# Table loads in two pieces that are split over the first tile, and each tile's sums folded on VectorE before one product of TensorE

## What is computed

```python
emb = embed_table[f_ix, x_idx]                       # n x 26 x 16
lin1 = w1_table[f_ix, x_idx].sum(axis=1, keepdims=True) + w1_bias
s = emb.sum(axis=1)
fm = 0.5 * ((s * s).sum(-1) - (emb * emb).sum(axis=(1, 2)))[:, None]
h = emb.reshape(n, F * D)
h = relu(h @ mlp_w1 + mlp_b1)
h = relu(h @ mlp_w2 + mlp_b2)
mlp_out = h @ mlp_w3 + mlp_b3
last = x0 = emb.transpose(0, 2, 1)
for W in (cin_w0, cin_w1, cin_w2):                   # three layers, K = 128
    last = einsum('ndl,ndf,klf->ndk', last, x0, W)
    feats.append(last)
cin_out = concatenate(feats, axis=-1).sum(axis=1)
return lin1 + fm + mlp_out + cin_out @ lin_w + lin_b
```

## Time and profile before

| | us |
|---|---|
| median of three runs | 621.58 (621.44 to 621.97) |
| the profiled execution's own time | 620.47 |
| its span, first to last instruction | 618.7 |
| TensorE busy | 495.0 (80%) |
| VectorE busy | 360.2 (58%) |
| ScalarE busy | 361.8 (58%) |
| GpSimd busy | 358.9 (58%) |

### The profile page before, as it was taken

One profiled execution on the slowest core, in us unless ns is written; L12 is line 12 of the kernel. 1 busy time (PEld: TensorE's weight loads), 2 busy tenths in 40 slices (PEclk: granted clock), 3 DMA queues, 4 the chain that ended last, 5 costly groups with the idle time before them and its releaser, 6 DMA issues. The chain is left out here.

```text
span 618.7 us, 7077 instructions
## 1 busy us (share of the span) xinstructions
PE 495.0 (80%) x2484; PEld 414.2 (67%) x2484; DVE 360.2 (58%) x587; ACT 361.8 (58%) x707; POOL 358.9 (58%) x379
## 2 busy tenths in 40 slices
PE   0986860000299999999999999999999999999998
PEld 0983550000188887878787878888888878787776
DVE  6710701010385858686867677685868686867556
ACT  0011701010476868686867778676868686867875
POOL 6777877730037777777777777777777777000000
PEclk9997575555599999999999999999999999999999
DMA  8944122210002222222222222222222222000000
GB/s 188 217 75 22 30 34 32 32 30 27 12 3 8 8 8 8 9 7 8 8 7 8 7 8 8 8 8 9 7 8 7 8 8 7 3 1 1 1 0 2
DMA packets 21365, 13.63 MB, mean 22 GB/s; under 512 B 12654, under 2 KB 20307, under 8 KB 21075
## 3 DMA queue, kind: packets, MB, share of 16 engines
q0 software_dynamic: 11968, 3.28, 15.4%
q1 hardware_dynamic: 5773, 7.92, 5.0%
q10 hardware_dynamic: 3590, 1.99, 1.7%
HBM read 12.97 MB, written 0.19 MB: 21 GB/s over the span
## 5 line engine op out<-in xcount | busy, mean ns | idle before, releaser
L412 POOL DMA_INDIRECT emb<-rows,idx_raw x374 | 358.5, 959 | 167.1 <-issue 117.2
L653 DVE TENSOR_TENSOR z_lo<-ps_s,z_hi 128x512 fp32r<-128x512 f32 (+1 forms) x192 | 132.0, 687 | 78.2 <-ACT ps_s L478 76.9
L471 ACT ACTIVATE z_hi<-ps_s 128x512 fp32r<-128x512 f32 (+1 forms) x192 | 114.2, 595 | 89.2 <-PE ps_s L888 88.3
L902 PE MATMUL ps_q<-z_lo,zw_hi 128*127 128x512 f32 (+1 forms) x192 | 85.9, 447 | 93.0 <-DVE z_lo L653 90.1
L478 ACT ACTIVATE ps_s<-ps_s 128x512 f32<-128x512 f32 (+1 forms) x192 | 114.0, 594 | 0.7
L902 PEld LDWEIGHTS ps_q<-z_lo,zw_hi 128*127 128x127 f32 (+1 forms) x192 | 36.6, 191 | 107.0 <-DVE z_lo L653 97.6
L903 PE MATMUL ps_q<-z_hi,zw_lo 128*127 128x512 f32 (+1 forms) x192 | 76.5, 398 | 0.0
L904 PE MATMUL ps_q<-z_hi,zw_hi 128*127 128x512 f32 (+1 forms) x192 | 76.2, 397 | 0.0
L888 PE MATMUL ps_s<-xt,pick 128*128 128x512 f32 (+1 forms) x192 | 74.7, 404 | 0.4 <-DVE xt L645 0.4
L980 PE MATMUL ps_y<-look_hi,one_hot 128*128 128x442 f32 (+1 forms) x168 | 61.1, 364 | 2.6 <-DVE one_hot L733 2.5
L981 PE MATMUL ps_y<-look_lo,one_hot 128*128 128x442 f32 (+1 forms) x168 | 59.3, 354 | 0.0
(11 more groups left out here) (165 smaller groups left out, 836.2 us busy)
## 6 DMA issues: line engine op xcount, KB each, us to landing
emb<-rows,idx_raw POOLq DMA_INDIRECT x374, 3.0
w_space<-rows SPq DMA_DIRECT2D x2, 826.5 KB
m_raw<-mlp_w SPq DMA_DIRECT2D x2, 650.0 KB
w<-cin_w SPq DMA_DIRECT2D x1, 832.0 KB, 6.8
w<-cin_w ACTq DMA_DIRECT2D x1, 832.0 KB, 13.4
w_space<-cin_w SPq DMA_DIRECT2D x1, 832.0 KB, 14.8
w_space<-cin_w ACTq DMA_DIRECT2D x1, 832.0 KB, 18.7
m_raw<-rows SPq DMA_DIRECT2D x1, 826.5 KB
```

Of the source, the lines that this page charges most:

```text
L412: pool.indirect_dma_start(emb[t % EMB][:, f, :], None, rows, bass.IndirectOffsetOnAxis(row_ix[:, t, f:f + 1], 0)).then_inc(gathered[t], 16)
L471: act.activation(z_hi[0:k, c, :], ps[0:k, :], ACT.Square)
L653: dve.tensor_tensor(z_lo[0:k, u % NC, :], ps_s[s_no(t, u) % RING][0:k, :], z_hi[0:k, u % NC, :].bitcast(F32), ALU.subtract).then_inc(lo_re ...
L902: pe.matmul(ps, hi_w, lo_x, start=(c == 0), stop=False)
```

## The change

- Each table's load goes in a DMA of 112 partitions and one of 15, in place of one of 127; the last partition stays by itself.
- The look-up by tables begins with tile 3 in place of 2 (FIRST_LOOK), so that tile 0 has no look work on TensorE and tile 2's three fields are gathered by GpSimd.
- ScalarE's table copies (`look_high`) stand behind chunks 4, 6 and 8 of tile 0, VectorE's (`look_low`) behind chunks 6, 8 and 10, no longer ahead of the tile. The copy `zw_hi` and its `zw_lo` stand ahead of tile 0's third square and `z_low`.
- `times_third` writes back into `ps_t`; a new `add_third` adds that to the sum of three quarters, ahead of the last `add_product`; a new `fold` sums the four blocks of 128 columns of `prod_sum` into `folded`. `sum_products` is one product of one column, which waits for `folds` and `looked`. TensorE's first use of `ps_t` in a tile waits for `tri_added` in place of `tri_prod`.
- The branches for a tile that isn't `joined` go; none of them ran but `copy_by_position(0)`'s and the last tile's, whose orders are kept.

```diff
+FIRST_LOOK = 3
...
-                sp.dma_start(look_raw[i][0:P - 1, :], rows[at:at + (P - 1) * COLS, :].rearrange(
-                    "(p c) r -> p (c r)", c=COLS)).then_inc(look_in[i], 16)
+                for r, r_end in ((0, 112), (112, P - 1)):
+                    sp.dma_start(look_raw[i][r:r_end, :], rows[at + r * COLS:at + r_end * COLS, :].rearrange(
+                        "(p c) r -> p (c r)", c=COLS)).then_inc(look_in[i], 16)
...
+            def look_high(i):
+                act.wait_ge(look_in[i], 48)
+                act.activation(look_hi[i][:], look_raw[i][:], ACT.Copy).then_inc(look_hi_ready, 1)
...
                     square(t, u)
+                    if t == 0 and u in LOOK_SPLIT:
+                        look_high(LOOK_SPLIT[u])
...
-            for u in range(NC):
-                square(0, u)
+            square(0, 0)
+            square(0, 1)
             act.wait_ge(za_done, 1)
             act.activation(zw_hi[:, 0, 0:NROW], ps_t[:, 0:NROW], ACT.Copy).then_inc(zw_hi_ready, 1)
-            for i in range(LOOKS):
-                act.wait_ge(look_in[i], 32)
-                act.activation(look_hi[i][:], look_raw[i][:], ACT.Copy).then_inc(look_hi_ready, 1)
+            square(0, 2)
...
-                dve.tensor_tensor(tri[:], ps_t[0:XK, :], x32[t % 2][:].rearrange("p c n -> p (c n)"),
-                                  ALU.mult).then_inc(tri_prod, 1)
+                dve.tensor_tensor(ps_t[0:XK, :], ps_t[0:XK, :], x32[t % 2][:].rearrange("p c n -> p (c n)"),
+                                  ALU.mult).then_inc(tri_prod, 1)
+
+            def add_third(t):
+                s = acc[(NQ - 2) % 2][0:XK, :]
+                dve.wait_ge(tri_prod, t + 1)
+                dve.wait_ge(q_bank_free, NQ * t + NQ - 1)
+                dve.tensor_tensor(s, ps_t[0:XK, :], s, ALU.add).then_inc(tri_added, 1)
+
+            def fold(t):
+
+                dve.wait_ge(q_bank_free, NQ * t + NQ)
                 if t:
                     dve.wait_ge(y_done, t)
+                dve.tensor_reduce(folded[0:NROW, :], prod_sum[0:NROW, :].rearrange("p (j n) -> p n j", j=QUAD), AX.X,
+                                  ALU.add).then_inc(folds, 1)
...
+                times_left(t - 1, NQ - 1)
+                times_third(t - 1)
+                add_third(t - 1)
                 z_low(t, 0)
+                add_product(t - 1, NQ - 1)
                 z_low(t, 1)
+                fold(t - 1)
+                hidden2(t - 1)
...
+            def look_low(i):
+                dve.wait_ge(look_hi_ready, i + 1)
+                dve.tensor_tensor(look_lo[i][:], look_raw[i][:], look_hi[i][:].bitcast(F32),
+                                  ALU.subtract).then_inc(look_lo_ready, 1)
...
             times_third(T - 1)
+            add_third(T - 1)
             times_left(T - 1, NQ - 1)
             add_product(T - 1, NQ - 1)
+            fold(T - 1)
...
-                for j in range(QUAD):
-                    pe.matmul(ps_y[:, YCOL + t:YCOL + t + 1], tri[:, j * P:(j + 1) * P], ones[0:XK, :],
-                              start=(j == 0), stop=False)
-                pe.wait_ge(q_bank_free, NQ * (t + 1))
-                for j in range(QUAD):
-                    mm = pe.matmul(ps_y[:, YCOL + t:YCOL + t + 1], prod_sum[0:NROW, j * P:(j + 1) * P], ones[0:NROW, :],
-                                   start=False, stop=(j == QUAD - 1))
-                mm.then_inc(y_done, 1)
+                if looked_during(t):
+                    pe.wait_ge(looked, looked_during(t))
+                pe.wait_ge(folds, t + 1)
+                pe.matmul(ps_y[:, YCOL + t:YCOL + t + 1], folded[0:NROW, :], ones[0:NROW, :],
+                          start=True, stop=True).then_inc(y_done, 1)
```

More of the change, by code:

```diff
@@ L168, in deepfm_cin_kernel @@
         prod_sum = sums[:, 2 * BANK:3 * BANK]
-        tri = sb("tri", [XK, BANK])
+        folded = sb("folded", [P, P])
         pick = sb("pick", [P, 2, sum(CK)], F32R)
@@ L297, in deepfm_cin_kernel @@
         quad_done, q_bank_free = sem("quad_done"), sem("q_bank_free")
-        third_done, prod_ready, tri_prod, y_done = sem("third_done"), sem("prod_ready"), sem("tri_prod"), sem("y_done")
+        third_done, prod_ready, y_done = sem("third_done"), sem("prod_ready"), sem("y_done")
+        tri_prod, tri_added, prod_added, folds = sem("tri_prod"), sem("tri_added"), sem("prod_added"), sem("folds")
         h1_done, h1_ready, h1t_done = sem("h1_done"), sem("h1_ready"), sem("h1t_done")
@@ L314, in looks, with looked_during @@
         def looks(t):
-            return LOOKS if LEAD <= t < T else 0
+            return LOOKS if FIRST_LOOK <= t < T else 0
         def look_no(t, i):
-            return LOOKS * (t - LEAD) + i
+            return LOOKS * (t - FIRST_LOOK) + i
+        def looked_during(t):
+            return LOOKS * max(0, min(t + LEAD, T - 1) - FIRST_LOOK + 1)
+        LOOK_SPLIT = {4: 0, 6: 1, 8: 2}
         KEYS = {1: 0, 5: 1, 9: 2}
@@ L324, in deepfm_cin_kernel @@
         PICKED = {5: 0, 9: 1}
-        def joined(t):
-            return 0 < t < T
         CONSTS = 15
@@ L487, in hidden1_high @@
                                ACT.Copy).then_inc(h1t_hi_ready, 1)
+            def look_high(i):
+                act.wait_ge(look_in[i], 48)
+                act.activation(look_hi[i][:], look_raw[i][:], ACT.Copy).then_inc(look_hi_ready, 1)
             def tile(t):
                 for u in range(NC, NU):
-                    if u == NU - 1 and joined(t + 1):
+                    if u == NU - 1 and t + 1 < T:
                         copy_by_position(t + 1)
                     square(t, u)
+                    if t == 0 and u in LOOK_SPLIT:
+                        look_high(LOOK_SPLIT[u])
                     if u == 5:
@@ L502, in start_tile @@
             def start_tile(t):
-                if not joined(t):
-                    copy_by_position(t)
                 x_high(t, 0)
@@ L669, in add_product @@
                 if q == 3:
+                    dve.wait_ge(tri_added, t + 1)
                     dve.wait_ge(q_bank_free, NQ * t + q)
                     if t:
-                        dve.wait_ge(y_done, t)
+                        dve.wait_ge(folds, t)
                 dve.tensor_tensor(sum_of(q)[0:NROW, :], ps_q[q % 2][0:NROW, :], acc[(q - 1) % 2][0:NROW, :],
@@ L703, in tile @@
                         hidden1_low(t)
+                    if t == 0 and u - 2 in LOOK_SPLIT:
+                        look_low(LOOK_SPLIT[u - 2])
                     if looks(t + LEAD):
@@ L710, in start_tile @@
             def start_tile(t):
[L711 to L715, removed]
                 x_low(t, 0)
                 x_low(t, 1)
-                if joined(t):
-                    times_left(t - 1, NQ - 1)
-                    times_third(t - 1)
+                times_left(t - 1, NQ - 1)
+                times_third(t - 1)
+                add_third(t - 1)
                 z_low(t, 0)
-                if joined(t):
-                    add_product(t - 1, NQ - 1)
+                add_product(t - 1, NQ - 1)
                 z_low(t, 1)
-                if joined(t):
-                    hidden2(t - 1)
+                fold(t - 1)
+                hidden2(t - 1)
                 if looks(t - 1 + LEAD):
@@ L794, in _ @@
                               zw_hi[LIN:LIN + F, 2, 0:NW].bitcast(F32), ALU.subtract).then_inc(zw_lo_ready, 1)
-            for u in range(NC):
-                z_low(0, u)
+            z_low(0, 0)
+            z_low(0, 1)
             dve.wait_ge(zw_hi_ready, 4)
@@ L799, in _ @@
                               ALU.subtract).then_inc(zw_lo_ready, 1)
[L800 to L803, removed]
+            z_low(0, 2)
             for t in range(T):
@@ L906, in main @@
                     if q == 0 and t:
-                        pe.wait_ge(tri_prod, t)
+                        pe.wait_ge(tri_added, t)
                     w = slice(LO * (1 - h), LO * (1 - h) + XK)
@@ L917, in sum_products @@
             def sum_products(t):
-                pe.wait_ge(tri_prod, t + 1)
-                if looks(LEAD + min(t, T - 1 - LEAD)):
-                    pe.wait_ge(looked, look_no(LEAD + min(t, T - 1 - LEAD), LOOKS))
-                for j in range(QUAD):
-                    pe.matmul(ps_y[:, YCOL + t:YCOL + t + 1], tri[:, j * P:(j + 1) * P], ones[0:XK, :],
-                              start=(j == 0), stop=False)
-                pe.wait_ge(q_bank_free, NQ * (t + 1))
-                for j in range(QUAD):
-                    mm = pe.matmul(ps_y[:, YCOL + t:YCOL + t + 1], prod_sum[0:NROW, j * P:(j + 1) * P], ones[0:NROW, :],
-                                   start=False, stop=(j == QUAD - 1))
-                mm.then_inc(y_done, 1)
+                if looked_during(t):
[3 more added lines that the diff above has]
+                          start=True, stop=True).then_inc(y_done, 1)
             def hidden1(t):
@@ L1026, in _ @@
                         picked(t, u + NC)
-                    if u == 1 and t and joined(t):
```

(5 more changed lines are left out.)

## The result

| | before | after |
|---|---|---|
| median of the runs, us | 621.78 (4 runs, 621.44 to 622.96) | 530.30 (4 runs, 530.12 to 530.45) |
| ratio after/before | | 0.8526 (95%: 0.8511 to 0.8541) |
| span of the profiled execution, us | 618.7 | 528.6 |
| TensorE busy | 495.0 (80%) | 468.6 (89%) |
| VectorE busy | 360.2 (58%) | 376.7 (71%) |

Forecast were 526.9 us and a range of 520 to 537. The time lies in the range, 3.4 us above the forecast value. The span is 4.6 us longer than the 524.0 that the sum gives. One run of the changed kernel further on (860.9 us) and one of the kernel before (942.9 us) were in a slower state, and no comparison uses them.

The account below looks back on a forecast made before the run. Two stages: serial table loads stall tile 0, then TensorE controls the tiles. Gains 81.5 + 1.5 + 10.8 + 1.5 - 0.6 = 94.7 us off 620.47 give 525.8, plus 1.1 for the runs' median: 526.9; range 520 to 537.

Parts of the forecast that it names:

- The hole: TensorE's idle stretch, 93 to 155 us, waiting on three serial table loads; removing it was to gain 81.5 us.
- doesn't spread: Rival: 112-row table loads still run in series at some 32 us, gain 13 in place of 81.5, 595.4 us; chance 0.05.
- Tile 0: First tile: ScalarE bounds it from 87.8 us, so tile 1's second `main` comes at 108.2 in place of 189.71.
- The fall of TensorE's clock to 1.2 GHz: Tile 0, TensorE idle between chunks: if the clock falls, products cost twice as much until it is back, 3 to 4 us.
- `add_third` on look tiles at nothing: VectorE, after `times_third`: the 0.69 us add fits in 1.09 us of idle time waiting for ScalarE, so costs 0.
- The fold: VectorE, after `z_low` 1: 0.69 us, delaying later operations by 0.6, leaving 0.83 us gain per boundary and not 1.6.
- the sign of being right: `first_all` from tile to tile 28.2 us apart in place of 29.05.
- The upper bound of 1.5 us: Boundaries after tiles 1 to 13: a strided fold costing 1.5 us rather than 0.7 would make the gain 0.
- VectorE takes all: Rival: the fold's stride or VectorE's longer row costs 0.8 us more per boundary, 537.7 us; chance 0.09.
- The end: After the last tile: eight product records of 1.05 us become 0.25, `add_third` and `fold` add 0.7 each; +0.6 us.
- the rival stayed away: Rival, gathers become the bound: at 1.30 us each in place of 1.248, the last lands at 498.5, 535.5 us; chance 0.07.
- the inference of the Trainium skill: GpSimd's gathers: a subtraction with two SBUF inputs doesn't hold up their descriptors; by that the lead would be 7.5 us.

Follow-up runs that it names:

- the experiment that would have told the forms apart: Changed kernel with table 0's `look_low` subtraction left out, table 1's replaced by a one-SBUF-input operation, table 2's kept: 845.9 us.

## Why the prediction was right, and where it was off, point by point

- *The hole is the series of one-engine loads.* Right, and shown by both halves: the pieces alone take 81 us off, the new order alone leaves tile 0 68 us late. One table's load moved 26 GB/s at a DMA share of 0.06 before, and 321 GB/s at 1.00 after. The Trainium skill's rule on how many engines share a DMA (DMA: Bandwidth & Descriptors, "Why a DMA increments its semaphore by 16 and not by 1") gives 1 for 127 rows and 16 for 112, and the traces agree with it. The rival "doesn't spread" is ruled out by the same rows. The loads were put much too late, at 81 and 90 us: they were over by 70 and 75, which changed nothing here, since the copies came at 82.98, 88.23 and 92.98.
- *Tile 0.* Forecast 108.2 for tile 1's second `main`, measured 107.46. ScalarE was the bound as put: its row has no idle from 84.5 to 101. The fall of TensorE's clock to 1.2 GHz, which stood only as a bound and as a sign of being wrong, did happen: TensorE was idle 1.96 us ahead of the product at 96.91, after gaps of 0.94 and 0.26, and the window 98 to 101 shows 0.59. From 98.56 to about 101.4 products start 0.42 us apart in place of 0.23. They lay beside ScalarE's and VectorE's rows, and cost 0.8 us at `x_high`. That the term came out is in part luck: chunk 3's `main` stood at 85.61 and not 86.5, as the clock was back at 2.4 GHz from about 81.5 on, where before it had been 84.5 and the forecast had put it no earlier; this 0.9 pays for the 0.8.

```profile
98.00:101.00 3.00, 3.00 (x12) 2.18 (x11) 3.00 (x4) 2.93 (x6) 2.39 (x3) 0.59 0.13 4
...
101.78 0.59 ACT L468 ACTIVATE x<-ps_s 52x512 f32<-52x512 f32 x1 [0.80 <-PE ps_s L898]
```

- *`add_third` on look tiles at nothing.* Right: VectorE's idle time ahead of `z_low` 0 fell from 1.09 to 0.49 and not below.
- *The fold.* This is the step that failed: "I take 0.69, 0.6 from start to start". It was 1.06 and 0.97. The mechanism was right, the fold does delay `looked` and `z_low` 2, but the term was mis-sized: 0.83 us per boundary forecast, 0.50 measured, and so 28.56 from `first_all` to `first_all` where 28.2 was the sign of being right. With the fold at 0.68 us, as it had been put, the period is 28.17, 0.88 less than before: the rest of the sum was sound. The row taken as nearest, L748, folds with a stride from PSUM; the new one folds from SBUF with a stride, and just this pair costs more. The upper bound of 1.5 us held it. TensorE's idle time ahead of chunk 2 stayed at 0.8, under the 1.5 that would have said that VectorE takes all.
- *The end.* Forecast +0.6, measured +1.35: the fold again (0.37), and a product of 0.56 us in place of 0.25. TensorE had been idle 3.6 us ahead of it.

```profile
525.88 0.56 PE L941 MATMUL ps_y<-ones,folded 127*128 127x1 f32 x2 [3.57 <-DVE folded L701]
```

- *Gathers.* The last was forecast to be there at 484.5; it was issued at 481.70 and so landed at about 484.7. Tile 15's copy came at 493.61, later than forecast by what the boundaries didn't give, so the lead was 8.9 us and the rival stayed away. All three table subtractions (line 749, at 88.96, 94.20 and 97.90) had a long gather beside them, and the ScalarE copy at 82.98 had none:

```profile
82.93 0.94 POOL L417 DMA_INDIRECT emb<-rows,idx_raw  x1 [0.30 <-issue]
...
89.17 2.49 POOL L417 DMA_INDIRECT emb<-rows,idx_raw  x1 [0.30 <-issue]
...
94.46 2.44 POOL L417 DMA_INDIRECT emb<-rows,idx_raw  x1 [0.30 <-issue]
...
98.45 2.15 POOL L417 DMA_INDIRECT emb<-rows,idx_raw  x1 [0.30 <-issue]
```

So the rows bear out going against the inference of the Trainium skill (SBUF — State Buffer, "Who interferes with whom") that was named in the prediction. That the two SBUF inputs are the cause is not shown: the coincidence speaks for it, and the experiment that would have told the forms apart had no gather beside them.

## What to carry to other kernels

Where an engine's copies wait for large DMAs in series, look first at the shape of the DMA and only then at the order: here the cut to 112 + 15 partitions was worth 81 us by itself, and the new order without it 7 us at tile 0. When work is moved from TensorE to VectorE at a place where both wait for each other, write down VectorE's row up to what TensorE waits for; only what is off that row is free, and a later place for the new operation can be worth more than the operation's length. Take the price of a new operation from a row with the same memory and the same stride together.

## What the runs showed of the hardware that was not expected

- A fold of 127x512 fp32 to 127x128 with a stride of 512 bytes takes 1.04 to 1.06 us from SBUF, 0.68 from PSUM, and 0.68 from SBUF without the stride.
- On the chips of the experiments TensorE, VectorE and ScalarE all stopped while gathers were being issued, the first two for "issue": 62 us without one instruction from 28 to 90 us, tiles of 44 to 47 us in place of 28.55. With one gather per tile in place of 23 the tiles were back at 28.5. The first runs had the same gathers and showed none of it.
- A load of 127 partitions in one DMA moved 26 GB/s at a DMA share of 0.06, one engine of 16; as 112 + 15 partitions it reached 321 GB/s at a share of 1.00.
